# Raw output weights in a buffer of their own, fetched seven steps sooner, and a new hand-written order for the end of the second layer and the first feed-forward rounds

## The chip, the cores and the metric

The kernel runs on one core of one Trainium2 chip. The metric is the device time of one execution in microseconds (us), the median of several runs. The profile is of one further execution, whose own time stands beside its span.

## What is computed

The reference is a stack of four sub-layers on x, two sequences (B = 2) of 512 tokens with 512 features, all in float32. Each adds a layer norm of its output to x, and works on a layer norm of x:

```python
x = x + _layernorm(_L0_attn_ref(_layernorm(x), Wq, Wk, Wv, Wo))          # 32 heads, 8 of K/V, rotary, causal
x = x + _layernorm(_L0_ffn_ref(_layernorm(x), lora_A, lora_B, W, bias))  # one linear map with 8 low-rank parts
x = x + _layernorm(_L1_attn_ref(_layernorm(x), Wq, bq, ..., gq, gk))     # 32 heads of 128, q and k RMS-normed
x = x + _layernorm(_L1_ffn_ref(_layernorm(x), w1, w3, w2, lora ...))     # silu(h1) * h3, 1376 hidden
```

The second attention, `_L1_attn_ref`, is the one around which the change lies: q, k, v = x W + b, an RMS norm of q and k per head, softmax(q k^T / sqrt(128)), times v, and the output projection `out @ Wo + bo`. The gated feed-forward `_L1_ffn_ref` follows it: h1 and h3 are products with 1376 hidden columns (here 11 tiles of 128), each with a low-rank addition, and a last product brings silu(h1) * h3 back to 512 features.

## The kernel before

**Products.** Every float32 operand is split into a high part `hi` and a rest `lo`, both in the fast float32 format, and `product` (lines 83 to 85) issues three matmuls for one: hi with lo, lo with hi, hi with hi. A high part is a copy by ScalarE (ACT), a rest a subtraction by VectorE (DVE) or GpSimd (POOL) in the helper at line 90. Five instruction streams, one for each engine and one for SyncE (SP), which issues every DMA, are ordered by semaphores.

**The second attention**, `paired_attention`, goes over 8 groups of 4 heads (one pass each), a group in two halves r = 0, 1 of 2 heads, and each half for both sequences: 8 slots (head, sequence) of 4 query tiles, 32 steps to a pass. A step n computes one 128x512 tile of scores on PE (`scores`), the row maxima on DVE (`tops`, line 1134), the exponentials on ACT (`exponentials`, line 958), and the 32x32 block transposes on DVE (`turn_blocks`, line 1149). Once a slot's four tiles are done, SP waits for the reciprocal sums (`inverses`, line 1140) and moves the blocks with 16 DMAs to their transposed places (`move`, line 757: `l_moved<-l_blocks`). ACT then copies the four chunks (`landed_hi`, line 964), POOL and DVE form the rests (`landed_lo`, line 90), and PE multiplies them with v (the use "pv", four chunks of three matmuls). DVE scales the result (`bank_use`, line 1104), ACT adds the bias of v (`output_hi`, line 976), DVE forms the rest (`output_lo`, line 1160), and PE applies the output weights (`project`), whose rows DVE adds to `acc` (`add_rows`, line 1167).

**Weights** come once for each half. Plans give the step of each event: `FETCH1` the SP loads, `LOADS1` the splits by ACT (`work`, line 932) and POOL. For the output weights ("wo", r) the load is at step 16 r + 11 and its two splits at 16 r + 13 and 16 r + 14; the load of the value weights ("wv", r) is at 16 r + 1. `raw_out` (2 tiles of 128x512 float32) shares its bytes with `w_out_lo`: the rest is written in place. So the load has to wait until PE has used the weights of the other half (line 718, a wait on `s_out`), and this wait stands in SP's stream ahead of the next slot's move.

**The closing.** From step 19 of the last pass on, the order on PE, ACT, DVE and POOL is written out by hand (`closing` in each of the four blocks); SP follows its plan to the end. PE computes the last 13 score tiles, the four last "pv" uses, the last four groups of projections, and in between merges the low-rank parts of the feed-forward weights (`entry.prepare`, lines 397 and 400) and transposes the first four token tiles (`entry.turn`, line 410). After the last scores and pv of slot 5 PE waits for every exponential (`s_exp`) ahead of the first `prepare`.

**The feed-forward rounds**, `swiglu_phase`: a round n handles hidden tile o for one sequence. PE computes h1 and h3 (24 matmuls, `ffn_h`), for the first sequence `prepare` of hidden tile o + 2 (parts 0 and 1), then `down` of the round before (12 matmuls, `ffn_rows`), then part 2 of `prepare`, then from round 3 a `turn`. A `prepare` waits until DVE has split the low-rank tile (`tile_lo`, line 452) and has added the part before the one before to the raw weights (`whole`, line 460), since two PSUM banks alternate. ACT turns a merged weight into its high part (`whole_hi`, line 422) and POOL into its rest (`whole_lo`). The second sequence enters in these rounds: `norm_attn` (sums of the attention rows), `root` on POOL (line 148), `center` on DVE (line 154), `scale_attn` on ACT (line 160), `add` to x on POOL (line 504), `sums` on DVE (line 133), then root, center, `scale`, and from round 3 `turn`. Rounds 0 to 2 have an order of their own in each stream; from round 3 on the rounds are alike.

Of the kernel before, what the change touches and what calls it, by code (L numbers as in the profile page):

```python
# [23 lines left out]
P = 128  # L24
# [263 lines left out]
FETCH1 = Plan({(kind, r): 16 * r + n for kind, n in (("wqk", -26), ("wv", 1), ("wo", 11)) for r in range(2)})  # L288
# [14 lines left out]
class Entry:  # L303
# [136 lines left out]
    def scalar_second(self, act, n):  # L440

        if TB <= n < TT:
            self.upper(act, n)
        for t in self.pair(n - 2):
            self.scale(act, t)
# [41 lines left out]
    def vector_second(self, dve, n):  # L487
        if TB <= n < TT:
            self.lower(dve, n)
        if n == 2:  # L490
            self.sums(dve, TT - 2)
            self.sums(dve, TT - 1)
        for t in self.pair(n - 2):
            self.norms.center(dve, FFN_IN, t)
# [11 lines left out]
    def gpsimd_second(self, pool, n):  # L506
        if n == 0:
            for t in range(TB, TT - 1):
                self.norms.root(pool, ATTN1, t)
            self.whole_lo(pool, 2, (0, 1))  # L510
            self.add(pool, TB)
            self.whole_lo(pool, 2, (2,))
            self.norms.root(pool, ATTN1, TT - 1)
            self.add(pool, TB + 1)
        elif n == 1:
            self.norms.root(pool, FFN_IN, TB)
            self.whole_lo(pool, 3, (0,))
            self.add(pool, TB + 2)
            self.whole_lo(pool, 3, (1, 2))
            self.norms.root(pool, FFN_IN, TB + 1)  # L520
            self.add(pool, TB + 3)
        elif n == 2:
            self.norms.root(pool, FFN_IN, TB + 2)
            self.norms.root(pool, FFN_IN, TB + 3)
# [96 lines left out]
def paired_attention(p, ctx0, xT, acc, ident, half, inv_rows, ahead, entry):  # L621
# [3 lines left out]
    with ExitStack() as ctx:  # L625
# [81 lines left out]
        def _(sp):  # L707
            def fetch(m, x, d):
                kind, r = x
                if not (m.first and d == 0 and r == 0) and m is not start:  # L710
# [5 lines left out]
                    else:  # L716
                        sp.wait_ge(s_out, m.done(OUTS1, (1 - r, 1, TB - 1), was))
# [204 lines left out]
        def _(act):  # L922
            def work(x, m, d):
# [5 lines left out]
                else:  # L929
                    per = (C if kind == "wv" else 2) * 16  # L930
# [75 lines left out]
            def closing(m):  # L1006
# [8 lines left out]
                exponentials(m, 19)  # L1015
                output_hi(m, 2)
# [3 lines left out]
                exponentials(m, 20)  # L1020
# [1600 lines left out]
```

## Time and profile before

| What | Value |
|---|---|
| Median of 3 runs | 2178.76 us (2177.76 to 2179.91) |
| The profiled execution's own time | 2179.0 us |
| Its span, first to last instruction | 2177.0 us |
| Busy: PE, DVE, ACT, POOL | 2081.8, 1631.3, 1349.1, 1229.1 us |
| Mean granted clock of TensorE over the span | 0.987 |
| Chain that ended last: PE, POOL, issue, DVE, ACT | 71%, 12%, 6%, 5%, 3% |

PE is matmul time, PEld its weight loads, SPq the DMA issues of SP's queue. "PEclk" is the granted clock as a share of full speed: 1.00 is 2.4 GHz and 0.50 is 1.2 GHz. In a timeline the bracket at a row's end is the idle time of that engine just before, and who ended it. Stages of the span: the first attention and its linear map to about 820 us, the second attention from there to its closing, which begins at about 1875 us, the feed-forward rounds from 1959.9 us.

### The profile page before, as it was taken

How to read it: one execution, taken by the hardware profiler on the slowest of the kernel's cores; microseconds unless marked ns; L12 is line 12 of the kernel's file. 1: busy time of each engine (PE TensorE's matmuls, PEld its weight loads, DVE VectorE, ACT ScalarE, POOL GpSimd, SP SyncE). 2: the span in 40 equal slices, each digit the busy share in tenths (PEclk: the TensorE clock that was granted, in tenths of full speed). 3: DMA queues.
4: the chain of work that ended last, by engine and by line, in shares of the span. 5: the costliest groups of instructions: out<-in, count | busy, mean ns of one | idle time of the engine just before them, and what ended most of it. 6: DMA issues, size and time to landing. Idle time of an engine off the chain costs nothing.

```text
span 2177.0 us, 37859 instructions
## 1 busy us (share of the span) xinstructions
PE 2081.8 (96%) x10535; PEld 1753.1 (81%) x10535; DVE 1631.3 (75%) x2969; ACT 1349.1 (62%) x3638; POOL 1229.1 (56%) x990
## 2 busy tenths in 40 slices
PE   6999999999999879999999999999999999978998
PEld 5788888888888657888888888888888888756787
DVE  6778888788888776878787777877777777865422
ACT  6877777777776555756566565666666565644321
POOL 3878778687786564546454554546454553445300
PEclk9999999999999989999999999999999999989999
DMA  2634444444444523555554455444544444652210
GB/s 84 142 98 127 106 108 117 109 113 121 111 112 131 133 74 68 110 118 116 114 109 102 115 116 117 104 101 116 116 110 100 119 109 92 147 127 82 88 54 25
DMA packets 219134, 231.69 MB, mean 106 GB/s; under 512 B 100528, under 2 KB 130384, under 8 KB 218992
## 3 DMA queue, kind: packets, MB, share of 16 engines
q1 hardware_dynamic: 218992, 229.97, 44.2%
q8 instruction: 67, 1.10, 0.3%
q14 instruction: 75, 0.61, 0.2%
HBM read 114.23 MB, written 6.55 MB: 55 GB/s over the span
## 4 chain that ended last, share of the span: by engine, by line
PE 71%; POOL 12%; issue 6%; DVE 5%; ACT 3%; DMA 1%; SPq 1%; POOLq 0%; DVEq 0%; ACTq 0%
PE l_general L83 13%; PE l_general L84 13%; PE l_general L85 13%; PE l_score L83 4%; PE l_out L83 4%; PE l_score L85 4%; PE l_out L84 4%; PE l_score L84 4%; PE l_out L85 4%; POOL l_rope L2255 3%; PE l_general L824 2%; POOL l_qT_lo L90 2%; POOL l_probsT_lo L90 2%; PE ffn_h L83 2%; PE ffn_h L84 2%
## 5 line engine op out<-in xcount | busy, mean ns | idle before, releaser
L90 POOL TENSOR_TENSOR l_probsT_lo<-l_moved,l_probsT_hi 128x512 fp32r<-128x512 f32 (+2 forms) x261 | 285.4, 1100 | 289.9 <-ACT l_probsT_hi L964 262.5
L958 ACT ACTIVATE l_probs<-l_score,l_negtop 128x512 f32<-128x512 f32 x256 | 176.0, 688 | 362.7 <-DVE l_negtop L1134 356.4
L90 DVE TENSOR_TENSOR l_probsT_lo<-l_moved,l_probsT_hi 128x512 fp32r<-128x512 f32 x251 | 282.7, 1126 | 30.4 <-ACT l_probsT_hi L964 29.9
L1134 DVE TENSOR_REDUCE l_negtop<-l_score 128x1 f32<-128x512 f32 x256 | 175.8, 687 | 92.9 <-PE l_score L85 90.2
L2057 ACT ACTIVATE l_probs<-l_score,l_negtop 128x128 f32<-128x128 f32 (+3 forms) x256 | 134.9, 527 | 170.4 <-DVE l_negtop L2170 169.1
L83 PE MATMUL l_score<-l_kT_lo,l_qT_hi 128*128 128x512 f32 (+3 forms) x512 | 190.7, 372 | 26.5 <-POOL l_qT_lo L90 9.0
L83 PE MATMUL l_out<-l_w_out_lo,l_oT_hi 128*128 128x512 f32 x512 | 208.2, 407 | 2.2 <-DVE l_oT_lo L90 2.2
L2170 DVE CUSTOM_DVE_ANT_0 l_score<-l_score,l_mask 128x128 f32<-128x128 f32 (+3 forms) x256 | 126.0, 492 | 107.9 <-PE l_score L85 106.6
L84 PE MATMUL l_out<-l_w_out_hi,l_oT_lo 128*128 128x512 f32 x512 | 201.0, 393 | 0.0
L85 PE MATMUL l_out<-l_w_out_hi,l_oT_hi 128*128 128x512 f32 x512 | 200.9, 392 | 0.0
L83 PE MATMUL l_general<-l_w_qk_lo,xT_hi 128*128 128x512 f32 x504 | 197.4, 392 | 0.0
L84 PE MATMUL l_general<-l_w_qk_hi,xT_lo 128*128 128x512 f32 x504 | 197.4, 392 | 0.0
L85 PE MATMUL l_general<-l_w_qk_hi,xT_hi 128*128 128x512 f32 x504 | 196.8, 390 | 0.0
L83 PE MATMUL l_general<-l_probsT_lo,l_v_hi 128*128 128x512 f32 (+3 forms) x512 | 182.3, 356 | 9.1 <-POOL l_probsT_lo L90 4.9
L85 PE MATMUL l_general<-l_probsT_hi,l_v_hi 128*128 128x512 f32 (+3 forms) x512 | 185.0, 361 | 0.0
L84 PE MATMUL l_general<-l_probsT_hi,l_v_lo 128*128 128x512 f32 (+3 forms) x512 | 184.7, 361 | 0.0
L85 PE MATMUL l_score<-l_kT_hi,l_qT_hi 128*128 128x512 f32 (+3 forms) x512 | 184.1, 360 | 0.0
L84 PE MATMUL l_score<-l_kT_hi,l_qT_lo 128*128 128x512 f32 (+3 forms) x512 | 183.5, 358 | 0.0
L1149 DVE STREAM_TRANSPOSE l_blocks<-l_probs 128x512 f32<-128x512 f32 x256 | 177.9, 695 | 7.0 <-ACT l_probs L958 7.0
L90 POOL TENSOR_TENSOR l_w_qk_lo<-l_raw_qk,l_w_qk_hi 128x512 fp32r<-128x512 f32 x60 | 77.8, 1297 | 151.0 <-ACT l_w_qk_hi L932 151.0
L607 ACT ACTIVATE l_squares<-l_y 128x128 f32<-128x128 f32 x512 | 151.9, 300 | 8.3 <-DVE l_y L1091 8.2
L964 ACT ACTIVATE l_probsT_hi<-l_moved 128x512 fp32r<-128x512 f32 x256 | 146.9, 629 | 10.1 <-DMA l_moved<-l_blocks 10.0
(251 smaller groups left out, 6237.3 us busy)
## 6 DMA issues: line engine op xcount, KB each, us to landing
l_moved<-l_blocks SPq DMA_DIRECT2D x1024, 64.0 KB
l_moved<-l_blocks SPq DMA_DIRECT2D x512, 80.0 KB
l_inv_all<-inv_rows SPq DMA_DIRECT2D x32, 512.0 KB, 4.3
l_raw_out<-l_wo SPq DMA_DIRECT2D x64, 256.0 KB, 4.4
l_inv_all<-inv_rows SPq DMA_DIRECT2D x64, 256.0 KB, 3.6
l_raw_q<-l_wq SPq DMA_DIRECT2D x32, 256.0 KB, 4.3
l_raw_qk<-l_wq SPq DMA_DIRECT2D x64, 128.0 KB, 2.9
l_raw_qk<-l_wk SPq DMA_DIRECT2D x64, 128.0 KB, 2.9
```

The source lines that it names most:

```text
L83: nc.tensor.matmul(out, left.hi, right.lo, start=first, stop=False, skip_group_check=True)
L84: nc.tensor.matmul(out, left.lo, right.hi, start=False, stop=False, skip_group_check=True)
L85: return nc.tensor.matmul(out, left.hi, right.hi, start=False, stop=last, skip_group_check=True)
L90: return engine.tensor_tensor(out, full, hi.bitcast(F32), ALU.subtract)
L607: last = act.activation(self.squares[:, h], self.y[:, b, t, h * HD:(h + 1) * HD], ACT.Square, accum_out=self.sumsq[:, b, j:j + 1])
L958: act.activation(probs[:, n % NPR], score[n % 2][:], ACT.Exp, bias=negtop[:, n:n + 1], accum_out=total[:, n:n + 1]).then_inc(s_exp, 1)
L964: act.activation(probsT_hi[:, :, k], moved[:, slot % 2, :, k], ACT.Copy).then_inc(s_land_hi, 1)
L1134: dve.tensor_reduce(negtop[:, n:n + 1], score[n % 2][:], AXX, ALU.max, negate=True)\
L1149: dve.transpose(to, probs[:, n % NPR]).then_inc(s_block, 1)
L2057: act.activation(probs[:, n % NPR, 0:width[t]], score[n % 2][:, 0:width[t]], ACT.Exp, bias=negtop[:, n:n + 1], scale=-1.0, accum_out=total ...
L2170: dve.tensor_tensor_reduce(out=score[n % 2][:, 0:w], in0=score[n % 2][:, 0:w], in1=mask[:, S - w:S], scale=-SCALE, scalar=3.0e38, op0=ALU. ...
L2255: pool.tensor_tensor(rope[:, r, 1], rope[:, r, 1], trig[:, 1], ALU.mult).then_inc(s_rope_add, 1)
```

## The change

It has four parts. (1) `raw_out` gets 2 x 512 floats per partition of its own, so that loading it no longer waits for PE. Its load moves from step 16 r + 11 to 16 r + 4, ahead of the move that starts at that step, and waits only for the splits of the half before; the wait for PE's projections moves to ACT, ahead of the first split of "wo". (2) In the closing ACT takes exponentials 20, 28, 29 and 30 sooner, splits the output weights before exponential 28, and copies the landed chunks of slots 4 and 5 later; one tile split moves to ACT's end. (3) DVE and POOL follow with an order of their own, and the copy of `b_v` is no longer the first thing that DVE does. (4) The feed-forward rounds 0 to 2 lose their own order and take that of the later ones; the entry of the second sequence is spread over one round more. PE's order is not touched.

```diff
-FETCH1 = Plan({(kind, r): 16 * r + n for kind, n in (("wqk", -26), ("wv", 1), ("wo", 11)) for r in range(2)})
+FETCH1 = Plan({(kind, r): 16 * r + n for kind, n in (("wqk", -26), ("wv", 1), ("wo", 4)) for r in range(2)})
...
         with ExitStack() as early:
             moved = p.sb(early, "l1_moved", [P, 2, TB, TB, P])
-            raw_out = p.sb(early, "l1_raw_out", [P, 2, D])
         probsT_lo = sb("probsT_lo", [P, 2, TB, TB, P], F32R)
         w_out_lo = sb("w_out_lo", [P, 2, D], F32R)
+        raw_out = sb("raw_out", [P, 2, D])
...
-                        sp.wait_ge(s_out, m.done(OUTS1, (1 - r, 1, TB - 1), was))
+                        sp.wait_ge(s_w, m.done(LOADS1, ("wo", 1 - r, 1), was))
...
+                    if kind == "wo" and j == 0 and not (m.first and d == 0 and r == 0):
+                        act.wait_ge(s_out, m.done(OUTS1, (1 - r, 1, TB - 1), d - (r == 0)))
+                        act.nop(nofuse=True)
```

The hand-written order of ACT in the closing:

```diff
                 landed(3, 0, 1, 2)
                 exponentials(m, 19)
+                exponentials(m, 20)
                 output_hi(m, 2)
...
-                exponentials(m, 20)
                 work(("wv", 1, 1), m, 0)
...
-                landed(4, 0, 1)
                 exponentials(m, 25)
                 bank_hi(("tq", 7), m, 0)
-                landed(4, 2, 3)
+                landed(4, 0, 1, 2, 3)
                 exponentials(m, 26)
                 bank_hi(("tk", 7), m, 0)
                 exponentials(m, 27)
-                landed(5, 0, 1)
+                work(("wo", 1, 0), m, 0)
+                work(("wo", 1, 1), m, 0)
                 exponentials(m, 28)
                 exponentials(m, 29)
+                output_hi(m, 4)
+                exponentials(m, 30)
+                landed(5, 0, 1)
+                exponentials(m, 31)
                 landed(5, 2, 3)
-                output_hi(m, 4)
-                work(("wo", 1, 0), m, 0)
                 entry.tile_hi(act, 1)
-                exponentials(m, 30)
-                work(("wo", 1, 1), m, 0)
-                exponentials(m, 31)
                 output_hi(m, 5)
...
+                entry.tile_hi(act, 2)
                 entry.whole_hi(act, 0, (2,))
```

DVE in the closing: the copy of `b_v` goes from first place to after `turn_blocks(m, 23)`; `tops` 19 and 20 go ahead of `turn_blocks` 18 and `bank_use(("pv", 2))`; `turn_blocks(m, 24)` goes up by three; `tops` 28 to 31 go ahead of `add_rows(m, (0, 1, 3), 0)`, the `tile_lo` and `landed_lo(m, 5, 3)`. POOL splits the output weights ahead of `landed_lo` of slot 5.

The feed-forward rounds, ACT and DVE (round n is hidden tile o of sequence b):

```diff
-                    if n == 0:
-                        entry.tile_hi(act, 2)
-                    if b == 0 and o >= 3:
+                    if b == 0 and o >= 1:
                         if o + 2 < HT:
                             entry.tile_hi(act, o + 2)
+                        if n == 1:
+                            entry.scale_attn(act, range(TB, TT - 1))
                         if o + 1 < HT:
                             entry.whole_hi(act, o + 1)
...
-                    if n == 0:
-                        entry.tile_lo(dve, 2)
-                        entry.norm_attn(dve, range(TB, TT - 1))
-                    elif n == 1:
-                        entry.sums(dve, TB)
-                        entry.whole(dve, 3, (0,))
-                        entry.sums(dve, TB + 1)
-                    if b == 0 and o >= 3:
+                    if b == 0:
                         if o + 2 < HT:
                             entry.tile_lo(dve, o + 2)
-                        if o + 1 < HT:
+                        if 2 <= o + 1 < HT:
                             entry.whole(dve, o + 1)
-                    if 2 <= n < TT:
+                    if n < TT:
                         entry.vector_second(dve, n)
```

What stood behind the gated product in rounds 0 and 1 on ACT and DVE (the rest of tiles 3 and 4 and of weights 2 and 3, and `norm_attn` and `scale_attn` of the second sequence) is gone from there. `vector_second` now takes `norm_attn` of tiles 4 to 6 in round 0 and of tile 7 in round 1, `sums` of tiles 4, 5 in round 2 and 6, 7 in round 3, and `center` one round after. ACT's `scale` follows one round later too. On POOL `gpsimd_second` now has in round 1 `whole_lo` of weight 2 around `root` of tile 7 and the first two `add`, in round 2 the other two `add` and the roots of tiles 4 and 5, and `whole_lo` of later weights starts with round 2.

## Rows read from the trace of the kernel before

**Rows 1.** The page, part 1 (busy time by engine) and part 2 (granted clock in 40 slices)

```profile
PE 2081.8 (96%) x10535; PEld 1753.1 (81%) x10535; DVE 1631.3 (75%) x2969; ACT 1349.1 (62%) x3638; POOL 1229.1 (56%) x990
...
PEclk9999999999999989999999999999999999989999
```

**Rows 2.** Windows: length; busy PE, PEld, DVE, ACT, POOL; PEclk; DMA share; GB/s

```profile
900.00:1780.00 880.00, 880.00 (x4643) 751.12 (x4642) 694.40 (x1050) 550.42 (x1716) 446.12 (x326) 1.00 0.49 111
...
1860.00:1960.00 100.00, 80.77 (x407) 67.04 (x406) 75.87 (x134) 50.58 (x101) 49.48 (x42) 0.91 0.61 139
...
2019.08:2029.53 10.45, 10.32 (x53) 8.16 (x51) 4.61 (x8) 4.00 (x8) 3.81 (x4) 1.00 0.80 274
```

**Rows 3.** Waits of PE from 1780 us to the end (total, times, longest)

```profile
PE l_score L83 <- ACT l_probs L958: 7.5, 3, 4.3
PE ffn_merge L400 <- DVE ffn_w_far_words L460: 7.3, 2, 5.8
PE ffn_merge L397 <- ACT l_probs L958: 6.4, 1, 6.4
PE l_general L83 <- POOL l_probsT_lo L90: 4.1, 1, 4.1
PE ffn_merge L400 <- DVE ffn_w_near_words L460: 2.6, 2, 1.5
PE ffn_merge L397 <- DVE ffn_tile L452: 0.9, 1, 0.9
```

**Rows 4.** Timeline of PE: start, duration, instruction [idle before it, releaser]

```profile
1899.83 0.39 PE L83 MATMUL l_general<-l_probsT_lo,l_v_hi 128*128 128x512 f32 x1
...
1924.12 1.11 PE L397 MATMUL ffn_merge<-ffn_tile,ffn_side 96*128 96x128 f32 x4 [6.39 <-ACT l_probs L958]
...
1959.90 0.50 PE L83 MATMUL ffn_h<-xT_lo,ffn_w_near 128*128 128x512 f32 x1
...
1995.75 0.77 PE L400 MATMUL ffn_merge<-ffn_side,ffn_tile 96*128 96x512 f32 x1 [5.75 <-DVE ffn_w_far_words L460]
...
2008.63 0.47 PE L83 MATMUL ffn_h<-xT_lo,ffn_w_far 128*128 128x512 f32 x1
```

**Rows 5.** Windows behind two of these waits, columns as in rows 2

```profile
1924.12:1928.90 4.78, 4.78 (x22) 4.78 (x23) 3.05 (x5) 0.56 (x1) 0.62 (x1) 0.50 0.15 24
...
1995.75:2000.70 4.95, 4.95 (x12) 3.96 (x13) 1.38 (x4) 3.15 (x5) 3.77 (x3) 0.51 0.62 192
```

**Rows 6.** Timeline of SyncE's DMA queue: a middle pass, then the closing

```profile
1526.90 2.32 SPq L728 DMA_DIRECT2D l_raw_v<-l_wv  x4
...
1535.56 10.04 SPq L757 DMA_DIRECT2D l_moved<-l_blocks  x16
...
1881.15 13.18 SPq L757 DMA_DIRECT2D l_moved<-l_blocks  x16
...
1896.17 10.58 SPq L757 DMA_DIRECT2D l_moved<-l_blocks  x16
...
1907.47 0.87 SPq L731 DMA_DIRECT2D l_raw_out<-l_wo  x2
```

**Rows 7.** Timeline of ACT: a middle pass, closing, third round

```profile
1550.57 1.14 ACT L964 ACTIVATE l_probsT_hi<-l_moved 128x512 fp32r<-128x512 f32 x2
...
1909.64 1.15 ACT L964 ACTIVATE l_probsT_hi<-l_moved 128x512 fp32r<-128x512 f32 x2 [7.22 <-DMA l_moved<-l_blocks]
...
1921.17 0.63 ACT L932 ACTIVATE l_w_out_hi<-l_raw_out 128x512 fp32r<-128x512 f32 x1 [7.40 <-DMA l_raw_out<-l_wo]
...
1990.19 1.52 ACT L160 ACTIVATE acc<-ffn_w_near_words,ffn_norm_bias,ffn_norm_rstd 128x512 f32<-128x512 f32 x2 [4.96 <-DVE ffn_norm_bias L154]
```

**Rows 8.** Timeline of DVE and POOL: closing, then second round

```profile
1876.61 0.75 DVE L1207 COPY l_b_v<-l_b_v_all 128x2 f32<-128x2 f32 x1
...
1896.50 5.49 POOL L90 TENSOR_TENSOR l_probsT_lo<-l_moved,l_probsT_hi 128x512 fp32r<-128x512 f32 x4 [11.37 <-ACT l_probsT_hi L964]
...
1971.39 2.84 POOL L90 TENSOR_TENSOR ffn_w_near<-ffn_w_near_words,ffn_w_near 128x512 fp32r<-128x512 f32 x2 [3.58 <-ACT ffn_w_near L422]
```

More of the change, by code:

```diff
@@ L443, in scalar_second @@
             self.upper(act, n)
-        for t in self.pair(n - 2):
+        for t in self.pair(n - 3):
             self.scale(act, t)
@@ L489, in vector_second @@
             self.lower(dve, n)
-        if n == 2:
-            self.sums(dve, TT - 2)
-            self.sums(dve, TT - 1)
+        if n == 0:
+            self.norm_attn(dve, range(TB, TT - 1))
+        elif n == 1:
+            self.norm_attn(dve, range(TT - 1, TT))
         for t in self.pair(n - 2):
+            self.sums(dve, t)
+        for t in self.pair(n - 3):
             self.norms.center(dve, FFN_IN, t)
@@ L509, in gpsimd_second @@
                 self.norms.root(pool, ATTN1, t)
+        elif n == 1:
             self.whole_lo(pool, 2, (0, 1))
+            self.norms.root(pool, ATTN1, TT - 1)
             self.add(pool, TB)
             self.whole_lo(pool, 2, (2,))
-            self.norms.root(pool, ATTN1, TT - 1)
             self.add(pool, TB + 1)
-        elif n == 1:
[L516 to L521, printed above, removed]
         elif n == 2:
-            self.norms.root(pool, FFN_IN, TB + 2)
-            self.norms.root(pool, FFN_IN, TB + 3)
+            self.add(pool, TT - 2)
+            self.add(pool, TT - 1)
+        for t in self.pair(n - 2):
+            self.norms.root(pool, FFN_IN, t)
 class Ahead:
@@ L1205, in scaled_output @@
                     bank_use(("pv", slot), m, 0)
-                dve.tensor_copy(b_v[:, 2:4], b_v_all[:, bass.ds(m.i * GH + 2, 2)]).then_inc(s_set, 1)
+                tops(m, 19)
                 turn_blocks(m, 18)
+                tops(m, 20)
                 bank_use(("pv", 2), m, 0)
-                tops(m, 19)
                 landed_lo(m, 3, 1)
-                tops(m, 20)
                 inverses(m, 4)
@@ L1227, in closing @@
                 turn_blocks(m, 23)
+                dve.tensor_copy(b_v[:, 2:4], b_v_all[:, bass.ds(m.i * GH + 2, 2)]).then_inc(s_set, 1)
                 entry.side_lo(dve, (0,))
@@ L1249, in closing @@
                 tops(m, 28)
-                add_rows(m, (0, 1, 3), 0)
-                entry.tile_lo(dve, 0)
                 tops(m, 29)
@@ L1354, in closing @@
                     landed_lo(m, 4, k)
+                work(("wo", 1, 0), m, 0)
+                work(("wo", 1, 1), m, 0)
                 for k in range(3):
                     landed_lo(m, 5, k)
-                work(("wo", 1, 0), m, 0)
-                work(("wo", 1, 1), m, 0)
                 landed_lo(m, 6, 0)
@@ L2495, in _ @@
                     rest(dve, gT.lo[:, n % NG3], gated[b], gT.hi[:, n % NG3]).then_inc(s_g_lo, 1)
-                    if n == 0:
-                        entry.whole(dve, 2, (0, 1))
-                        entry.tile_lo(dve, 3)
-                        entry.whole(dve, 2, (2,))
-                        entry.norm_attn(dve, range(TT - 1, TT))
-                    elif n == 1:
-                        entry.whole(dve, 3, (1, 2))
-                        entry.tile_lo(dve, 4)
             dve.wait_ge(s_back[1], TB * 16)
```

28 lines of the change are left out of this document (10 added, 18 removed).

## The prediction, made before the changed kernel ran

> **What bounds the kernel now.** I read the busy shares first. PE is busy 2081.8 us of 2177.0, so at most 95 us can be won, and none beside PE [rows 1]. The clock string has dips only at the start, at about 800 us and near the end [rows 1]. The windows say where PE stands still: in 880 us of the second attention it is busy 880.00 us at a clock of 1.00, so nothing that the change does in the loop can gain. The closing has 19.2 idle us in 100, at a mean clock of 0.91, and a steady feed-forward round again almost none, 10.32 busy of 10.45 [rows 2]. All the change can win lies between 1875 and 2009 us. The list of PE's waits there adds up to 28.8 us [rows 3]. Four are long: 6.4 for the last exponential, 5.8 for a merged weight, 4.3 for an exponential, 4.1 for the rests of slot 7. Behind two of them stands a second price: the granted clock is 0.50 or 0.51 (the 1.2 GHz level) for 4.78 and 4.95 us of PE work [rows 5], which costs about half of each, 2.4 and 2.5 us, after PE had stood still for 6.39 and 5.75 us [rows 4].
>
> The other streams say why. ACT stands 7.40 us before the split of the output weights and has exponentials 30 and 31 queued behind it; it was released by the load `l_raw_out<-l_wo` [rows 7]. SP issued that load at 1907.47, only after slot 5's move [rows 6], as its wait for PE's projections demanded. Before that, ACT stands 7.22 us for slot 5's blocks with exponentials 28 and 29 behind [rows 7]. In feed-forward round 2 ACT stands 4.96 us for a center of the second sequence, ahead of that round's silu [rows 7]. On it hang the gated product, its two parts, `tile_lo`, `whole`, and PE's wait of 5.75 [rows 4].
>
> **Part 1, the load, in the loop.** Two issues (0.87 us) [rows 6] move to behind the value weights' load. There SP's queue shows 1526.90 + 2.32 = 1529.2, then nothing until shortly before the move at 1535.56: the issues fit. That move takes 10.04 us, ends at 1545.6, and ACT uses the blocks at 1550.57 without a wait [rows 6, 7]. The new SP wait, for splits half a pass old, is met and holds nothing up; behind it stands slot 0's or 4's move. The new wait on ACT is for projections three steps earlier in PE's order; behind it stand the split and the next exponential. ACT is busy 550 of 880 us there and PE never waits [rows 2]. All 15 repeats: 0. If this cover went, each late microsecond of a move or an exponential would be paid 15 times (rival D). Upper bound of a gain in the loop: 0, as PE has no idle time to give.
>
> **Parts 1 to 3, the closing.** The load now goes out before slot 4's move, some 29 us sooner, so even its 13 us there (1907.9 to 1921.17) end before ACT wants it near 1905. The new wait on ACT, for projection (0,1,3), holds exponential 28; but PE computes scores 28 only after that same projection, so it costs 0, or at most the two splits (2 x 0.63) that now stand ahead of it. Both long waits for exponentials lose their causes. What is late next is the blocks. Slot 4's move took 13.18 us and slot 5's 10.58, back to back [rows 6]. They start when `inverses(4)` has run, which no longer has the 0.75 us copy of `b_v` ahead of it [rows 8]: slot 5's blocks land at about 1909.0 instead of 1909.64. The early microseconds (exponential 19 sooner, no wait ahead of score 21) mostly go back at pv of slot 4: PE would be there 3 us before 1899.83 [rows 4], but POOL's four rests run from 1896.50 to 1902.0 [rows 8], and they hang on the landing. The same for slot 5: 1909.0, + 0.6 for a first copy (half of 1.15), + 4.1 for three of the four rests at 5.49, + 0.7 for exponential 31, which now stands between the copies (about the 0.63 of a tile on ACT), + 1.2 for the last chunk (3 of 12 matmuls that took 4.95 us at half clock) [rows 5] = 1915.6. Then nothing holds the first `prepare`, which stood at 1924.12 [rows 4]: 8.5 us. The 4.78 us behind it run at full clock: 2.4 more. PE's own broken wait for slot 5 (about 3 us before the first chunk) will probably lower the clock once, between 0 and 2.5 us [rows 5]; I take 1.6, since the wait is shorter than those two, but not by much. **Closing: 8.5 + 2.4 - 1.6 = 9.3 us**, bounds 3 and 12.5. The tail has the same order and hangs on exponential 31 and SP. Its wait of 4.1 stays [rows 3]. Slot 6's move loses the load ahead of it, slot 7's can start right behind; with 10 to 13 us each they just keep up.
>
> **Part 4, the rounds.** PE's first `ffn_h` is at 1959.90, round 4's at 2008.63: 48.7 us for four rounds [rows 4]. What they need: 10.45 for a full round [rows 2]; rounds 1 and 2 have no transposes and no bank wait, about 0.9 less each; round 0 in addition no `down` (12 matmuls, some 2.5 at full clock) [rows 5] and no part 2 (0.5): 6.6 + 9.55 + 9.55 + 10.45 = 36.1. New waits, walked in the new order: in round 1 `whole` of weight 2 comes behind round 0's gated product and the split of tile 3, so part 2 of `prepare` waits some 2.2 us instead of 1.5. Then POOL has two rests (2.84) [rows 8] ahead of the root of tile 7, DVE's center waits for it, and the gated product stands behind: 1.9 instead of 1.5. In round 2 no silu waits for the second sequence any more. DVE reaches `whole` of weight 4 about 28.9 us after the first `ffn_h`, PE wants it at 29.1: the 5.8 and the 0.9 go [rows 3], and the slow 4.95 with them. So 36.1 + 4.1 = 40.2, a gain of 8.5. Added up by waits it is 5.8 + 0.9 + 2.5 - 0.7 - 0.4 = 8.1. **Rounds: 8.5 us**, bounds 3 and 10. Later rounds keep their rows.
>
> **Sum.** 2179.0 (the profiled execution's own time, 0.2 over the median of 2178.76) - 9.3 - 8.5 = **2161.2 us**, forecast 2161.
>
> **Rivals.** *A, the blocks take the exponentials' place.* Slot 4's or 5's move lands later than I have it, and PE gives back at slot 5 what it had. For it: both moves are on my path and ran 10 to 13 us. Against: the load is then out of the way of slot 6. Closing gain 3: 2179.0 - 3 - 8.5 = 2167.5. *B, the rounds keep a wait.* The margin at `whole` of weight 4 is 0.2 us; a little more work on DVE or POOL brings part of the wait back. Gain there 4: 2165.7. Both together: 2172. *C, the clock.* The windows show 1.2 GHz only behind long stands [rows 5], and my walk puts several short ones in their place. If each of two more groups (slot 4, rounds 1 and 2) lowers the clock at 2.0 to 2.5 us, it is 2161 + 4.5 = 2165.5. The Trainium skill (TensorE: Matmul & The Clock Gate, "A second HAM failure mode") says that a PE that pauses briefly but often between groups swings between the two levels; by that rule this rival is the forecast. *D, slower.* The load now runs just ahead of the moves of slots 0 and 4. If it makes the blocks land later than ACT uses them, in the loop, PE waits in each of 15 halves. That needs 5 us (the gap from 1545.6 to 1550.57) less the landing time; from 1.5 us of wait per half it turns the sign: 15 x 1.5 = 22.5 against 17.8, so 2183.7. Against: SP's gap before that move and PE's 880.00. The Trainium skill (DMA: Bandwidth & Descriptors, "Issuing engines are not separate DMA queues") has all transfers interleave on the same 16 engines, which speaks for D; no row shows a load next to a move that cost PE anything. *E, more.* One of slot 4's issues held SP for 3 us over the 10.04 of a plain move [rows 6]; if the stall falls elsewhere now, slot 5 lands sooner: 2158. *F, nothing measurable:* both gains are eaten by waits that I don't see. A measurement of this kernel can tell 0.2% (4.4 us) from no change, so this is 2174.4 to 2183.1.
>
> **Chances.** Forecast 0.52, A 0.13, B 0.10, C 0.08, A and B 0.03, E 0.07, F 0.04, D 0.03. Faster is all but F and D: 0.93; same 0.04; slower 0.03. The range takes in the forecast's bounds, E, A, B and C: 2155 to 2170. It leaves out F, D, A with B, and the far ends of the terms.
>
> **What would show it.** Right: no wait of ACT for `l_raw_out`; the first `ffn_merge` some 8 us sooner; the stretch behind it at a clock of 1.00; a new wait of PE for `l_probsT_lo` of POOL at slots 4 and 5; the wait of 4.1 unchanged; from the first `ffn_h` to round 4 about 40 us with two waits near 2; the loop still 880 of 880 us busy. Wrong: PE waits in the loop (D), a wait above 3 us in rounds 1 to 3 (B), slot 5's blocks after 1912 us (A), more than two dips of the clock behind the start of the closing (C).

## The result, and the profile after

The changed kernel takes 2169.27 us (median of 6 runs, 2167.0 to 2171.16), the kernel before 2178.81 (6 runs beside them): 9.5 us less, a ratio of 0.9958 with a 95% interval of 0.9948 to 0.9969. The forecast was 2161, from 2155 to 2170: the sign and the range hold, the gain is about half of the forecast 17.8 us. Two repeats on other chips gave 2170.72 and 2172.16 us, ratios of 0.9969 and 0.9970 (experiments 1 and 6). By these three the gain lies between 6 and 10 us. The profiled execution's own time is 2171.16, its span 2169.2.

The page of the changed kernel, busy time by engine and granted clock in 40 slices, answers to [rows 1]:

```profile
PE 2081.9 (96%) x10535; PEld 1751.8 (81%) x10535; DVE 1629.3 (75%) x2969; ACT 1349.3 (62%) x3638; POOL 1230.4 (57%) x990
...
PEclk9999999999999989999999999999999999999999
```

PE does the same work; the dip near the end of the clock string, a mean over 54 us, is gone. The windows answer to [rows 2], with one for the rounds added; in the kernel before, that window had 40.22 us busy in 50 at a clock of 0.93:

```profile
900.00:1780.00 880.00, 880.00 (x4643) 751.06 (x4642) 694.63 (x1048) 547.65 (x1710) 446.97 (x326) 1.00 0.50 111
1860.00:1960.00 100.00, 83.60 (x437) 68.41 (x436) 80.31 (x141) 56.19 (x120) 52.15 (x44) 0.95 0.63 145
1960.00:2010.00 50.00, 45.06 (x215) 36.44 (x214) 31.78 (x65) 24.16 (x40) 29.93 (x28) 1.00 0.29 89
```

The loop is as full as it was. The rounds have 4.9 idle us in 50 where they had 9.8. But the closing has 16.4 idle us in 100, only 2.8 fewer than before. PE's list of waits from 1780 us on, against [rows 3], says why:

```profile
PE l_general L83 <- POOL l_probsT_lo L90: 13.3, 6, 7.5
PE ffn_merge L400 <- DVE ffn_w_near_words L460: 3.3, 2, 2.3
PE ffn_merge L400 <- DVE ffn_w_far_words L460: 2.5, 1, 2.5
PE l_score L83 <- ACT l_probs L960: 1.3, 2, 0.9
```

The waits for exponentials fell from 13.9 us (7.5 + 6.4) to 1.3. In their place stand waits for the rests of moved blocks, 13.3 in place of 4.1. The longest, 7.5 us, is new.

**Where the time went.** Absolute times of two executions can't be subtracted here, since the changed kernel's second attention began 5.2 us late (below). So I cut each profile at four marks. M is the start of the row maxima of step 16 of the last pass (before: 1862.12). The closing runs from M to the first `ffn_h` (1959.90 in [rows 4]), the rounds from there to the start of round 4 (2008.63), the tail from there to the end of the span. On DVE, M of the changed kernel is this row:

```profile
1867.28 0.69 DVE L1136 TENSOR_REDUCE l_negtop<-l_score 128x1 f32<-128x512 f32 x1 [1.29 <-PE l_score L85]
```

| us | M | M to first prepare | closing | rounds | tail | span |
|---|---|---|---|---|---|---|
| before | 1862.1 | 62.0 | 97.8 | 48.7 | 168.4 | 2177.0 |
| changed | 1867.3 | 58.8 | 92.3 | 41.4 | 168.3 | 2169.2 |
| difference | +5.2 | -3.2 | -5.5 | -7.4 | -0.1 | -7.8 |

The rounds came as forecast (7.4 of 8.5). The closing gave 5.5 of 9.3, and a late start took 5.2 back.

**The late start.** The first maxima of the second attention start at 836.93 before and 842.08 after, and M at 1862.12 and 1867.28: from the one to the other both kernels take 1025.2 us. So the 5.2 us arose before the loop. Between 745 and 810 us the mean granted clock was 0.87 before and 0.79 after, which fits a part of it; the change touches nothing that runs there. Over all 14 profiles of this study the first maxima start between 836.9 and 842.3; the four without the early load have a mean of 839.8, the ten with it of 840.0. So the scatter comes with and without the change. What starts it isn't shown. The profile on which I forecast had the earliest start of all.

**Why the closing gave less.** First the moves of the changed kernel on SP's queue:

```profile
1884.44 0.85 SPq L730 DMA_DIRECT2D l_raw_out<-l_wo  x2
1885.92 12.84 SPq L756 DMA_DIRECT2D l_moved<-l_blocks  x16
1900.60 10.38 SPq L756 DMA_DIRECT2D l_moved<-l_blocks  x16
1912.60 10.02 SPq L756 DMA_DIRECT2D l_moved<-l_blocks  x16
```

The load goes out ahead of slot 4's move and no engine waits for it. Then ACT from 1910 to 1919 us. Its first row waits 4.63 us for PE's projection, the wait that the change moved to ACT; exponential 28 behind it began when its maxima were there, so this cost nothing:

```profile
1910.24 1.15 ACT L934 ACTIVATE l_w_out_hi<-l_raw_out 128x512 fp32r<-128x512 f32 x2 [4.63 <-PE l_out L85]
...
1915.60 0.69 ACT L960 ACTIVATE l_probs<-l_score,l_negtop 128x512 f32<-128x512 f32 x1 [1.94 <-DVE l_negtop L1136]
...
1916.28 1.14 ACT L966 ACTIVATE l_probsT_hi<-l_moved 128x512 fp32r<-128x512 f32 x2
1917.38 0.69 ACT L960 ACTIVATE l_probs<-l_score,l_negtop 128x512 f32<-128x512 f32 x1
...
1918.06 1.14 ACT L966 ACTIVATE l_probsT_hi<-l_moved 128x512 fp32r<-128x512 f32 x2
```

and DVE and POOL beside it:

```profile
1914.28 0.71 DVE L1151 STREAM_TRANSPOSE l_blocks<-l_probs 128x512 f32<-128x512 f32 x1 [2.04 <-DMA l_moved<-l_blocks]
...
1921.63 0.66 DVE L90 TENSOR_TENSOR l_probsT_lo<-l_moved,l_probsT_hi 128x512 fp32r<-128x512 f32 x1
...
1916.97 4.48 POOL L90 TENSOR_TENSOR l_probsT_lo<-l_moved,l_probsT_hi 128x512 fp32r<-128x512 f32 x3 [3.51 <-ACT l_probsT_hi L966]
```

Slot 5's blocks landed at 1914.2: DVE's transpose into the same buffer is released by that landing at 1914.28. Less the 5.2 us of late start that is the 1909.0 of the forecast. But ACT copies the first of them only at 1916.28. It is not idle for want of blocks: the new order puts exponential 30 ahead of the copies, exponential 30 needs its maxima, and on DVE the maxima of step 30 stand behind the transpose of step 28, which itself has to wait for slot 5's move, because it writes the buffer which that move reads. PE shows what follows:

```profile
1921.60 0.77 PE L83 MATMUL l_general<-l_probsT_lo,l_v_hi 128*128 128x512 f32 x1 [7.52 <-POOL l_probsT_lo L90]
...
1926.09 0.56 PE L397 MATMUL ffn_merge<-ffn_tile,ffn_side 96*128 96x128 f32 x4
...
1971.24 0.47 PE L400 MATMUL ffn_merge<-ffn_side,ffn_tile 96*128 96x512 f32 x1 [2.29 <-DVE ffn_w_near_words L460]
...
1980.71 0.47 PE L400 MATMUL ffn_merge<-ffn_side,ffn_tile 96*128 96x512 f32 x1 [2.53 <-DVE ffn_w_far_words L460]
```

The four chunks of a slot are numbered 0 to 3; chunks 0 and 2 are the even ones. In the last pass PE's first chunk of slot 5 waits for both even rests (the `pieces` of line 831 in the kernel before), that is for the last of POOL's three. So all 12 matmuls come after 1921.6, 4.5 us of them up to the first prepare. The forecast had counted only the last three behind the last rest.

### The profile page after: what moved, and what is told of

Same layout as the page of the kernel before. It is cut to its first block, busy times and chain, and to the rows that moved or that the text cites. A ratio compares the mean times of both kernels' runs of the same rounds, so it can differ in the third digit from the quotient of the medians.

```text
span 2169.2 us, 37874 instructions
## 1 busy us (share of the span) xinstructions
PE 2081.9 (96%) x10535; PEld 1751.8 (81%) x10535; DVE 1629.3 (75%) x2969; ACT 1349.3 (62%) x3638; POOL 1230.4 (57%) x990
## 3 DMA queue, kind: packets, MB, share of 16 engines
q1 hardware_dynamic: 218992, 229.97, 44.3%
## 4 chain that ended last, share of the span: by engine, by line
PE 71%; POOL 12%; issue 6%; DVE 4%; SPq 3%; ACT 2%; DMA 1%; POOLq 0%; DVEq 0%; ACTq 0%
PE l_general L83 13%; PE l_general L84 13%; PE l_general L85 13%; PE l_score L83 4%; PE l_out L83 4%; PE l_score L85 4%; PE l_score L84 4%; PE l_out L84 4%; PE l_out L85 4%; POOL l_rope L2257 3%; PE l_general L823 2%; POOL l_probsT_lo L90 2%; POOL l_qT_lo L90 2%; SPq L756 2%; PE ffn_h L83 2%
## 5 line engine op out<-in xcount | busy, mean ns | idle before, releaser
L2059 ACT ACTIVATE l_probs<-l_score,l_negtop 128x128 f32<-128x128 f32 (+3 forms) x256 | 134.9, 527 | 168.3 <-DVE l_negtop L2172 167.5
L1327 POOL TENSOR_TENSOR l_y<-l_y,l_meansq 128x512 f32<-128x512 f32 x128 | 148.0, 1184 | 2.5
```

Source lines behind the costliest of these rows:

```text
L1327: pool.tensor_tensor(rows, rows, by, ALU.mult).then_inc(s_yn, 1)
L2059: act.activation(probs[:, n % NPR, 0:width[t]], score[n % 2][:, 0:width[t]], ACT.Exp, bias=negtop[:, n:n + 1], scale=-1.0, accum_out=total ...
```

## Experiments

Each kernel is told with its own spans. Groups of four ran on one chip each, and the ratios are to the kernel before on the same chip. "Closing" and "rounds" are the stretches defined above, each from one profile. The intervals of the ratios are 0.2 to 0.3% (4 to 7 us) wide, so the medians tell less than the stretches.

**1. One part at a time.** For these runs I cut the change into three: the load (part 1 of the change), the closing order (parts 2 and 3) and the rounds (part 4). The load: a home of its own and step 4 in place of 11, with its two waits. The closing: the hand-written orders of ACT, DVE and POOL in the last pass. The rounds: the order of rounds 0 to 2. I put in the load alone, the rounds alone, and both with the closing order left as before.

```diff
 # load_only, load_rounds
-(("wqk", -26), ("wv", 1), ("wo", 11))
+(("wqk", -26), ("wv", 1), ("wo", 4))
+        raw_out = sb("raw_out", [P, 2, D])
-                        sp.wait_ge(s_out, m.done(OUTS1, (1 - r, 1, TB - 1), was))
+                        sp.wait_ge(s_w, m.done(LOADS1, ("wo", 1 - r, 1), was))
```

> Only part 1: raw_out in a buffer of its own, its load at step 16r+4, the wait for the projections on ACT. Closing and feed-forward rounds as before. Theory 1 (the load alone frees the exponentials, and the new closing order takes some of it back): ACT's 7.4 us wait for raw_out goes, exponentials 30 and 31 follow straight behind slot 5's copies, the first prepare starts right behind pv of slot 5 (6.4 us sooner) and the 4.8 us behind it run at 2.4 GHz (2.4 more): the stretch from the maxima of step 16 of the last pass to the first ffn_h is 97.8 - 8.7 = 89.1 us, against 92.3 in the changed kernel; median about 2170. Rival (the new order earns the closing's gain): the stretch stays at 92.3 or above, median 2173 or above. The loop keeps its period in both.

> Only part 4: the new order of the feed-forward rounds (with its tile split at ACT's end of the closing). Both theories: from the first ffn_h to round 4's 41.4 us instead of 48.7, as in the changed kernel, closing 97.8 as before, median 2178.8 - 7.4 = 2171.4. If it differs from 41.4 by over 1 us, the rounds' gain depends on how the closing ends.

> Parts 1 and 4 without the new order of the closing. Theory 1: gains add, 8.7 + 7.4 = 16.1: 2162.7, faster than the changed kernel by 3 us in the stretch of the closing. Rival: the load without its order gains at most 5.5, so 2166 or above.

> The changed kernel once more. In its first profile the second attention began 5.2 us later than in that of the kernel before, in code that the change does not touch. Theory 1 (chance: such stretches differ from execution to execution with the phase of the clock): the maxima of step 16 of the last pass start somewhere between 1860 and 1868 us here, and scatter the same way in the kernels of this call whether they have the new load or not. Rival (the change causes it): 1867 +- 0.5 here and in load_only and load_rounds, 1862 +- 0.5 in rounds_only. Time 2167 to 2171; closing 92.3 and rounds 41.4 again.

| kernel | median us | ratio, 95% interval | M | closing | rounds |
|---|---|---|---|---|---|
| load alone | 2175.14 | 0.9985 (0.9976 to 0.9994) | 1865.3 | 89.7 | 49.1 |
| rounds alone | 2172.86 | 0.9971 (0.9960 to 0.9982) | 1866.9 | 94.5 | 42.9 |
| load and rounds | 2168.88 | 0.9951 (0.9937 to 0.9965) | 1865.9 | 90.9 | 42.9 |
| all of the change | 2170.72 | 0.9969 (0.9953 to 0.9986) | 1866.2 | 91.9 | 41.4 |

The load alone had the stretch that I expected (89.7 for 89.1) but not the time: 2175.14 for 2170, on the rival's side of 2173. Load and rounds missed theirs as well, 2168.88 for 2162.7, where the rival had said 2166 or above. Both forecasts were made against the closing of 97.8, which was a long one (experiment 2). The rounds alone took 42.9 us and not 41.4, over the 1 us by which I would have held that their gain depends on how the closing ends; but a later profile of the changed kernel itself took 43.0, so this difference doesn't speak for that.

Load and rounds together are as fast as the whole change, the intervals overlap. The new closing order on top of the early load wins nothing: with the old order the closing took 89.7, 90.9 and 89.7 us (the third in experiment 6), with the new one 92.3, 91.9, 94.0 and 91.8 (experiments 4 and 6), in the mean 2.4 more. In the load alone, ACT copies slot 5's blocks at once when they land, and finds the output weights there behind them:

```profile
1911.52 1.15 ACT L967 ACTIVATE l_probsT_hi<-l_moved 128x512 fp32r<-128x512 f32 x2 [6.35 <-DMA l_moved<-l_blocks]
...
1913.90 1.14 ACT L967 ACTIVATE l_probsT_hi<-l_moved 128x512 fp32r<-128x512 f32 x2
...
1915.55 0.62 ACT L935 ACTIVATE l_w_out_hi<-l_raw_out 128x512 fp32r<-128x512 f32 x1
```

That is 46.2 us after its M; in the changed kernel it is 49.0 (1916.28 less 1867.28). The 7.40 us of ACT in [rows 7] are gone by the load alone.

**2. The kernel before once more.** To see how far one profile of before can be trusted, I took another.

> The kernel before once more, for its profile. Theory 1 (its first profile was one draw of two things that scatter: the start of the last pass, and how long the late load of the output weights takes to land): the maxima of step 16 of the last pass between 1862 and 1868 us, and from there to the first ffn_h 94 to 98 us, as in rounds_only (94.5), not always 97.8; the rounds 48.7. Rival: 1862.1 and 97.8 again within 0.5, and then the 5 us later start in every variant is owed to something that all variants share.

Its time was 2178.27, M 1864.0, the closing 95.2, the rounds 48.8. ACT waits for the late load here too, but less:

```profile
1921.00 0.63 ACT L932 ACTIVATE l_w_out_hi<-l_raw_out 128x512 fp32r<-128x512 f32 x1 [6.09 <-DMA l_raw_out<-l_wo]
```

From the load's issue to this copy are 12.5 us (1908.46 to 1921.00), 13.7 in the profile of [rows 6, 7] and 10.9 with the new rounds alone. So 97.8 was a long closing of the kernel before, and 1862.1 an early M; the two nearly cancel in the span. With the 94.5 of the rounds alone, which has the late load and the old order too, the mean of three is 95.8.

**3. Slot 5's copies first.** If the theory of the closing holds, ACT should copy slot 5's blocks ahead of exponentials 30 and 31, and DVE do its one rest of slot 5 sooner. A second kernel also starts the first even chunk after one piece.

```diff
                 output_hi(m, 4)
+                landed(5, 0, 1, 2, 3)
                 exponentials(m, 30)
-                landed(5, 0, 1)
                 exponentials(m, 31)
-                landed(5, 2, 3)
...
                 tops(m, 31)
+                landed_lo(m, 5, 3)
                 output_lo(m, 4)
-                entry.tile_lo(dve, 0)
                 turn_blocks(m, 30)
                 turn_blocks(m, 31)
                 inverses(m, 7)
-                landed_lo(m, 5, 3)
+                entry.tile_lo(dve, 0)
...
 # landed5_pieces in addition
-                        pieces = TB // 2 if m.last and slot == SLOTS - 3 else k // 2 + 1
+                        pieces = TB // 2 if m.last and slot == SLOTS - 3 and k % 2 else k // 2 + 1
```

> The changed kernel, but ACT copies all four chunks of slot 5 ahead of exponentials 30 and 31, and DVE takes its rest of slot 5 straight after the maxima of tile 31. Theory 2 (exponential 30 hangs on slot 5's move through the block transposes of slot 7, which need the buffer that the move empties, and holds the copies 2.1 us; the last odd rest stands behind four other things on DVE): pv of slot 5 starts 2 to 2.5 us sooner, the stretch of the closing 92.1 - 2.3 = 89.8, median 2 us under the changed kernel. Rival (POOL's three rests or the landing itself set the start): under 0.5 us.

> The same, and PE's first chunk of slot 5 waits for one even piece instead of both. Theory 2: the first chunk starts 2.5 us sooner again, and the end of pv comes 1 to 2 us sooner than in landed5_first, since the chunks are then paced by POOL's rests of 1.3 us each; closing 88 to 89. Rival: several short waits in place of one keep or put the clock at 1.2 GHz and nothing is won over landed5_first.

They took 2167.87 and 2167.93 us, both with the ratio 0.9948 (0.9935 to 0.9961). The closing fell to 90.0 and 89.5 us. PE's waits in the second show that the 7.5 us are broken up:

```profile
1915.23 0.47 PE L83 MATMUL l_general<-l_probsT_lo,l_v_hi 128*128 128x512 f32 x1 [1.80 <-POOL l_probsT_lo L90]
...
1916.93 0.80 PE L83 MATMUL l_general<-l_probsT_lo,l_v_hi 128*128 128x512 f32 x1 [0.77 <-DVE l_probsT_lo L90]
...
1920.93 0.95 PE L397 MATMUL ffn_merge<-ffn_tile,ffn_side 96*128 96x128 f32 x4
```

The first prepare is 56.4 us after M in the first kernel and 53.9 in the second (its M is 1867.01), where it was 58.8; the forecast had 53.5. The cause of the shortfall there is thus shown: the order of the copies with DVE's rest (2.4 us), and the piece rule (2.5). At the first `ffn_h` the order still brings 2.3 us, but the piece rule only 0.5, so its closing is half a microsecond longer than the 88 to 89 that I expected. Its PE ran at a granted clock of 0.50 from 1917 to 1923 us, past the first prepare, and again from 1941 to 1947, where the changed kernel had 0.61 and 0.82 behind the same wait for slot 7. My rival, that several short waits put the clock at 1.2 GHz and nothing is won, is thus nearly what happened: the two medians are equal.

The rounds took 44.3 and 43.0 us where the changed kernel's took 41.4. They hold the same two waits of 2.3 and 2.6 us in all of them; what differs is the clock (below). The intervals of both ratios overlap with the changed kernel's, so the time alone doesn't show a gain.

**4. A shorter wait in the rounds.** POOL had two rests ahead of the root of tile 7 in round 1; now it has one.

```diff
-            self.whole_lo(pool, 2, (0, 1))
+            self.whole_lo(pool, 2, (0,))
             self.norms.root(pool, ATTN1, TT - 1)
+            self.whole_lo(pool, 2, (1,))
```

> The changed kernel, but POOL takes the root of tile 7 after one rest of weight 2 instead of two. Theory 3 (in round 1 the gated product stands behind DVE's center of tile 7, and that behind POOL's second rest): PE's wait of 2.5 us in round 1 falls to about 1.2, the four rounds 41.4 - 1.3 = 40.1. Rival (the gated product waits for h3 or ACT's silu): rounds 41.4 as before.

2168.32 us, ratio 0.9956 (0.9944 to 0.9968), rounds 40.3 us. In PE's list the wait that was 2.5 is

```profile
PE ffn_merge L400 <- DVE ffn_w_far_words L460: 1.5, 1, 1.5
```

against the 1.2 and rounds of 40.1 that I expected. It confirms the cause that the forecast gave for this wait: two rests ahead of that root.

**5. The new closing order without the early load.**

> The new closing order without the early load: the output weights are still loaded ahead of slot 6's moves, as before. My theory: the new order needs the early load. ScalarE copies the output weights ahead of exponentials 28 to 30, and in the three profiles with the late load they were there 56.4 to 59.1 us after the start of the last step's maxima, where the changed kernel began that copy at 43.0; the copies of slot 5 follow 6 us behind it, so they begin at 62 to 65 in place of 49, the first prepare comes 9.8 us later at 72 to 75, the closing stretch takes 105.7 to 108, the rounds 48.7 as before: 2186 to 2190 us, slower than before by about 10. Rival: ScalarE's place for the copy doesn't matter, because the slot's own move sets the start: closing stretch 92 to 95, 2173 to 2176 us.

2188.26 us (5 runs), ratio 1.0042 (1.0029 to 1.0055): slower than the kernel before by 10.1, closing 105.5, rounds 48.9, as the theory had it (105.7 to 108, 48.7). First a row of ACT, then PE's waits from 1880 us to 2020:

```profile
1923.47 1.15 ACT L932 ACTIVATE l_w_out_hi<-l_raw_out 128x512 fp32r<-128x512 f32 x2 [19.01 <-DMA l_raw_out<-l_wo]
```

```profile
PE l_score L83 <- ACT l_probs L958: 15.3, 2, 15.0
PE l_general L83 <- POOL l_probsT_lo L90: 10.8, 5, 5.5
```

The new order has the output weights ahead of exponentials 28 to 30, so everything behind them stands for 19 us. The order needs the load; the load doesn't need the order.

**6. The edits together.** The first kernel is the changed one with the edits of 3 and 4 (copies, piece rule, root); the second has load and rounds with the old closing order and the root's edit; the third is the changed kernel on the same chip.

> The changed kernel with three more edits: slot 5's blocks copied ahead of exponentials 30 and 31, its first even chunk started after one piece, and the root of tile 7 one rest earlier. Theory: the first two edits take the closing stretch to 89.5 us (measured with them), the third shortens the second wait of the rounds from 2.5 to 1.5 us, and with it the clock dip that the rounds had behind those two edits (42.97 us) doesn't come: rounds 40.3 us. Against the changed kernel's 92.3 and 41.4 that is 3.9 us less: about 2166 us, 12 to 13 below the kernel before. Rival: the dip depends on where the first wait of 2.3 us falls, not on the second's length: rounds stay at 42 to 43, and the time is 2167.5 to 2168, as with two edits.

> Early load and new rounds with the old closing order, and the root of tile 7 one rest earlier. With the old closing order the rounds had taken 42.9 us against 41.4 behind the new one, the same waits of 2.3 and 2.6 us but the clock at 0.89 and 0.94 in two stretches of 10 us. Theory: closing stretch 90.9 us as before this edit, second wait 1.5 us, no dip, rounds 40.3: about 2166.3 us. Rival: the dip stays, rounds 41.9, about 2168 us.

> The changed kernel once more, on the chip of these runs, for the comparison with the two above: 2169 to 2171 us, closing stretch 91.9 to 92.3 us, rounds 41.4 us.

| kernel | median us | ratio, 95% interval | M | closing | rounds |
|---|---|---|---|---|---|
| changed, with three edits | 2164.25 | 0.9938 (0.9926 to 0.9950) | 1863.6 | 89.6 | 40.3 |
| old closing order, load, rounds, root | 2166.57 | 0.9947 (0.9934 to 0.9960) | 1865.5 | 89.7 | 40.3 |
| changed | 2172.16 | 0.9970 (0.9959 to 0.9982) | 1867.8 | 94.0 | 43.0 |

The rounds of the first two came to 40.3 us as expected, without a dip of the clock; the closing of the first as expected too, that of the second 1.2 us shorter. The changed kernel's own third profile missed all that I expected of it: closing 94.0, rounds 43.0, median 2172.16. With all three edits the kernel is faster than the changed one on the same chip, by 7.9 us, twice the 3.9 expected; the intervals of the ratios lie apart (0.9950 against 0.9959). It has the lowest median of this study, but the old closing order with load, rounds and root is within its interval, at 2.3 us more. PE's waits and windows of that version:

```profile
PE l_general L83 <- POOL l_probsT_lo L90: 7.8, 5, 4.1
PE ffn_merge L400 <- DVE ffn_w_near_words L460: 3.3, 2, 2.3
PE ffn_merge L400 <- DVE ffn_w_far_words L460: 1.5, 1, 1.5
```

```profile
1860.00:1960.00 100.00, 88.30 (x453) 72.38 (x452) 81.50 (x147) 56.28 (x110) 56.41 (x47) 0.93 0.64 148
1960.00:2010.00 50.00, 45.99 (x217) 36.61 (x216) 28.73 (x58) 23.84 (x40) 27.84 (x25) 1.00 0.36 118
```

The 4.1 us ahead of slot 7 are the longest wait left in the closing. The old closing order gets the same 89.7 us without any of these edits to it.

## Why the prediction was right in sign and range, and twice too high in size

- **The bound** held: outside of the closing and the rounds next to nothing moved by the change. One reading ahead of it was wrong and carried nothing: the clock string of [rows 1] has no dip at the start, only the two at about 800 us and near the end.
- **Luck in the range.** The closing fell short by almost 4 us and the median still lay in the range, 0.7 us below its upper end; the two repeats of the changed kernel, 2170.72 and 2172.16, lie above 2170.
- **The loop's term of 0** was right within a microsecond, and **rival D** showed in miniature. From the first maxima to M the four profiles without the early load took 1025.0 to 1025.2 us, the ten with it 1025.2 to 1026.5, in the mean 0.6 more. Eight of the ten have a wait of PE for moved blocks in the first pass, once or twice, of 0.17 to 0.35 us, the other profiles none, and nowhere in the passes behind it. Two of them, in the kernel with the piece rule changed:

```profile
885.18 0.49 PE L83 MATMUL l_general<-l_probsT_lo,l_v_hi 128*128 128x512 f32 x1 [0.33 <-POOL l_probsT_lo L90]
...
955.64 0.50 PE L83 MATMUL l_general<-l_probsT_lo,l_v_hi 128*128 128x512 f32 x1 [0.33 <-POOL l_probsT_lo L90]
```

  The run with the load alone has such a wait too, 0.34 us, so it comes with part 1. That the load's transfer delays the blocks isn't shown. Slot 0's move of the first pass took 11.5 to 12.1 us of SP's queue in the ten profiles and 10.5 to 10.9 in the four, although the load had gone out 28 us before it and the DMA engines stood idle in between (share 0.00 to 0.02). Slot 4's, 7 us behind a load in the ten, took 13.1 to 15.8 in the ten and 13.2 to 13.8 in the four. From the second pass on the cover that I named holds. The Trainium skill (DMA: Bandwidth & Descriptors, "Issuing engines are not separate DMA queues") has all transfers interleave on the same 16 engines. The price in the loop is 0.6 us here and not the 22.5 of the rival, and no row ties even that to the sharing.
- **The load's theory** held: no wait of ACT for it, issue ahead of slot 4's move, no price for the two new waits in the closing, slot 5's blocks 46.9 us after M in both the forecast (1909.0 less 1862.1) and the trace (1914.2 less 1867.3). **Rival A**, late blocks, is out: the blocks came after 1912 us only because all of the last pass began 5.2 us late; against M they were on time, and yet the first prepare moved by 3.2 us only. Its time, 2167.5, is nearer to the measured one than mine, but not by its mechanism. **Rival E**, a stall that falls elsewhere, is out too: slot 4's move took 12.84 us where it had 13.18.
- **The step that failed** is the chain behind the landing, "+ 0.6 for a first copy ... + 1.2 for the last chunk ... = 1915.6". It lacks two things. The copies did not start at the landing but 2.1 us later (1916.28 against 1914.2), because exponential 30 stands ahead of them and hangs over DVE on the same landing. And PE waits for both even rests with its first chunk, so 12 matmuls follow the wait and not 3: 4.5 us (1921.60 to 1926.09) where I had 1.2, at half clock in part. Together 2.1 + 3.3 = 5.4, the 5.3 us between the forecast 8.5 and the measured 3.2. Of the 4.5 us some 1.9 is the dip of the clock, which the sum had as a term of its own, at 1.6; without it the chain is 3.5 us short, most of the 3.8 between the forecast closing gain of 9.3 and the measured 5.5. I had walked ACT's queue and not what its items wait for on DVE, and read the piece rule as that of the other slots. PE's wait for slot 5 is 7.5 us where I had "about 3". The wait of 4.1 ahead of slot 7 stayed, at 4.08. Experiment 3 shows both causes: with the copies ahead and the piece rule changed the first prepare stands at 53.9 us behind M, where the sum had 53.5.
- **The clock terms** of the closing held: 2.3 us more were won behind the first prepare (5.5 less 3.2) against 2.4. The forecast dip of 1.6 came at slot 5: 12 matmuls in 4.7 us (to 1926.26) where 12 at the 0.23 us of those ahead of the wait take 2.8, which is 1.9.
- **The rounds** held but for one term: waits of 2.29 and 2.53 us where 2.2 and 1.9 were worked out, the two behind them gone, 41.4 us against 40.2. The second wait was taken 0.6 too small. **Rival B** is out, no wait was above 3.
- **Rival C**, more dips of the clock, is half right. In the profile of the result it did not happen: behind the closing's start the clock fell at slot 5 and at slot 7, two groups, and the rounds ran at 1.00. In the third profile of the same kernel it fell in the rounds as well. The Trainium skill (TensorE: Matmul & The Clock Gate, "A second HAM failure mode") tells of such swings in a PE that pauses often between groups. Its case is another kernel in bf16; here the same pauses brought a dip in some executions and none in others.
- **The base.** The sum was made against one profiled execution whose closing was 97.8 us; the second one had 95.2. Against the mean of the two (96.5) the closing of the changed kernel, 92.8 as the mean of its three profiles, gains 3.7 and not 5.5. The rounds gain 48.8 less 41.9, 6.8 us. The sum of 10.5, less the 0.6 of the loop, is near the 9.5 between the medians. One profile's start scatters by 5 us, as much as a part of the change is worth; the stretches between marks scatter less.
- **The load alone** is nearly accounted for. With the old order, the closing is 95.8 us in the mean of three profiles with the late load and 90.1 in three with the early one, 5.7 less. Less the 0.6 of the loop and the 0.3 by which its rounds are longer that is 4.8, and the interval of its ratio takes in 1.3 to 5.2 us.

## What to carry to other kernels

A late load that holds an in-order engine is worth removing first, and it may carry all that a rewrite of the order around it seems to bring: try the parts alone. Here the load and the rounds carried the gain, and the new closing order gave back 2.4 us of its stretch. When a wait is taken away, walk the chain of the next releaser item by item, each with the engine that it in turn waits for, and read how many instructions stand behind the last wait, not how many need its last piece. An order by hand that puts work for step 30 ahead of data that has landed ties the data to step 30's own chain.

## What the runs showed of the hardware that was not expected

**The same short waits lower the clock or don't.** The rounds of seven profiles hold the same two waits, 2.3 us and 2.5 to 2.6 us. Two of them (both of the changed kernel) took 41.4 us, at a clock of 1.00. Four took 42.9 to 43.0 and one 44.3, each with a stretch at the lower level behind the second wait. In the changed kernel's third profile the fall stands right behind the second wait. These windows are of its rounds:

```profile
1980.00:1983.00 3.00, 0.43 (x3) 0.03 (x1) 2.94 (x4) 0.11 (x1) 1.72 (x2) 1.00 0.00 0
1983.00:1986.00 3.00, 3.00 (x8) 2.35 (x9) 2.66 (x6) 1.74 (x3) 2.41 (x2) 0.53 0.73 190
1986.00:1989.00 3.00, 3.00 (x13) 2.46 (x12) 0.35 (x3) 0.60 (x1) 3.00 (x4) 0.90 0.34 122
```

PE stood for 2.57 us, then ran at the lower level (0.53 in a window is nearly all 1.2 GHz) for some 3 us, which costs 1.6. With the second wait at 1.5 us, three profiles of three kernels took 40.3 us in the rounds and had a clock of 1.00. So a wait of this kernel of some 2.5 us costs 2.5 us, or some 4.1, once 5.4, and cutting it by 1.0 us saves that and, in the three profiles that there are, the dip. What makes the difference between two equal waits isn't shown.

**One load landed late, in the last pass only.** From its first issue to the copy that waited for it the last load of the output weights (2 x 256 KB) took 10.9, 11.9, 12.5 and 13.7 us in the four profiles that issued it behind slot 5's move. The page and a window on the closing of the kernel before give the median from issue to landing, of all such loads of both attentions and of the last two:

```profile
l_raw_out<-l_wo SPq DMA_DIRECT2D x64, 256.0 KB, 4.4
...
l_raw_out<-l_wo SPq DMA_DIRECT2D x2, 256.0 KB, 9.3
```

The 15 loads at the same place of the loop, behind one move and ahead of the next, are 30 transfers in each of these four profiles, and all landed 2.5 to 6.7 us after their issue. In the first of them the next move was issued 1.5 us behind the load, as in the closing, and they took 4.6 to 6.2. Of the last load's two transfers one took 4.1 to 5.4 us and the other 10.5 to 13.2. So a move right behind the load doesn't by itself make it late; what does isn't shown. Issued seven steps sooner in the last pass, ahead of slot 4's move, the slower of the two still took 5.8 to 10.4 us in the ten profiles, but nothing waited for it. The first load of the changed kernel, beside the value weights' alone and no move, landed 3.9 and 4.3 us after the issue. The Trainium skill (DMA: Bandwidth & Descriptors, "Anatomy of one DMA — SWDGE (gpsimd) path") gives for GpSimd's path 2.0 us and the bytes at 436 GB/s; by that 2 x 256 KB would take about 3.2 us, an estimate. These loads are issued by SyncE, and the rows are above it.
